# Keys and values projected side by side, outputs moved to the keys' bank, and the engines' orders rewritten, in a fused attention, recurrence and experts layer

## The chip, the cores and the metric

The kernel runs on one core of one Trainium2 chip. The metric is the device time of one execution in microseconds. TensorE, VectorE, ScalarE, GpSimd and SyncE each run their own program; semaphores alone order them.

## What is computed

Three residual stages on 128 sequences of 32 tokens with 256 channels: cross attention over a context of 257 positions per sequence, a short recurrence (its part for sequence 0 is used for all), and a mixture of eight experts of which each token takes two.

```
x = x + xattn(layernorm(x), ctx, mask)       # 16 heads of 16
x = x + attn(layernorm(x), W_in, conv, ...)  # out = Y[0] / norm, norm from cumsums of A * softplus(dt)
x = x + ffn(layernorm(x), router, gate, up, down)

q = hidden @ Wq.T + bq;  k = enc @ Wk.T + bk;  v = enc @ Wv.T + bv
scores = q k / sqrt(16) + mask;  out = softmax(scores) v;  return out @ Wo.T + bo
h = silu(xf @ w_gate[e]) * (xf @ w_up[e]);  out += gates[:, e] * (h @ w_down[e])
```

## The kernel before

The first part (`attend`) covers attention, recurrence and routing, the second (`experts`) the 71 slots of 128 tokens of the experts. The change lies in the first.

A tile is 128 tokens: four sequences, called batches or steps 0 to 3; there are 32 tiles and 128 batches. In step (i, b), batch n = 4i + b, every engine works at several depths: scores and softmax are those of batch n+1, keys and values those of n+2, the split of the context into two parts is that of n+3, and the output is that of n. What follows attention for a whole tile (`i-1`, `i-2`, `i-3`: output projection, norms, softplus, decays, router, ranks) is cut into pieces that hang on a step's number. Tiles 4 to 28 run in a loop on TensorE, the others are unrolled (`steps`, line 278); the order is written out by hand in a function `tile` for each engine (lines 664, 804, 1143, 1291).

TensorE's step before: `scores` of n+1, `project_k` of n+2, `turn_a`, `weigh_values` of n, the first half of `transpose_probs` of n+1, `turn_b`, `project_v` of n+2, the second half of the transposes, `turn_c`. Keys and values are each twelve matmuls of 256 columns of the split (fp32r) type; the others are of 32-bit type. The pieces: `turn_a` is `expand`, `turn_y`, `queries`, `router` for b = 0 to 3; `turn_b` is `sum_decay_and_rank`, `project_y`, `project_dt`, `turn_z1`; `turn_c` is `project_out`, `turn_z2`, `turn_z3`, `sum_a`. All of them write the bank `M`, so each waits until the piece before has been read.

The eight banks of the matmul's memory: `K` (keys), `V_` (values), four `SC` (scores by group), `PT` (transposed probabilities), `M`. The outputs `OT` and the row sums `RP` lie at the end of `SC[0]` (line 228). So scores of n+1 wait for the outputs of n-1 to be taken (`ou_done`, `rp_done`), and weighing waits for the maximum of group 0. Both halves of the transposes use `PT`: the second waits until ScalarE has copied the first.

VectorE: `maxima` (line 879, four per step: scores plus mask, with their row extremum), `take_keys` (868), `take_output` (892, 894), `reciprocals`, and the small operations of the later stages; the softplus is a chain of operations on `dtv` (lines 964 to 984), each waiting for the one before, and ends in `a_done`, for which `sum_a` on TensorE waits. ScalarE: `split_high`, `exponentials` (735), `take_probs`, `take_values`, `take_rp` and the copies out of `M` (711). GpSimd: `split_low` (1249), `lay_queries`, `last_probs` (1267, 1271), the inverse square roots (`power`, 1231 and 1233), table writes. SyncE loads contexts, masks and inputs and is not changed.

## Time and profile before

| | us |
|---|---|
| median of 3 runs | 1527.64 |
| lowest and highest | 1525.33 and 1528.30 |
| the profiled execution | 1529.16 |
| its span | 1527.2 |
| TensorE busy, matmul | 1422.5 (93%) |
| VectorE busy | 1125.5 (74%) |
| ScalarE busy | 1000.9 (66%) |
| GpSimd busy | 838.1 (55%) |
| mean granted TensorE clock | 0.969 of full |

The first scores start at 19.5 us, the last at 956.5; the first expert slot's matmuls start at 1016.5. Between 80 and 110 us the recurrence of sequence 0 is computed once, with TensorE mostly idle. Busy shares are averages over these stages. In the timelines below a line is a run of like instructions: start, busy length, engine, line, operation, output<-inputs and the count; in brackets the idle time ahead of it and what ended it. A matmul's length goes past the start of the next, so the distance of two starts is what a block costs.

### The profile page before, as it was taken

Reading aid. Unit: us, or ns where it says so; the run is one execution under the profiler, and the core shown is the slowest. Engines: PE = TensorE matmul, PEld = TensorE weight load, DVE = VectorE, ACT = ScalarE, POOL = GpSimd, SP = SyncE. Lnnn points to the kernel's source line nnn. Section 1 sums busy time; section 2 is a strip of 40 time slices with the busy share of each in tenths; the row PEclk is TensorE's granted clock in tenths of the full one; section 3 lists DMA queues with packets and bytes.
Section 4 is the critical chain, followed back from the end, with each engine's and each line's share of the span. In section 5 each row is a group of like instructions: output and inputs, shape, how many; then the busy total and the mean of one; then the engine's idle time right before and its main releaser. Section 6 shows DMA issues by size and latency. Waiting matters only on the chain.

```text
span 1527.2 us, 53971 instructions
## 1 busy us (share of the span) xinstructions
PE 1422.5 (93%) x15668; PEld 1294.9 (85%) x15669; DVE 1125.5 (74%) x3967; ACT 1000.9 (66%) x2482; POOL 838.1 (55%) x1401
## 2 busy tenths in 40 slices
PE   6969999999999999999999999649999999999997
PEld 5858888888888888888888888449999999999997
DVE  3647777777777777777777777557877787787775
ACT  4726766767766766766766676237777777677674
POOL 4514655655655655565565554226665666566554
PEclk9969999999999999999999999569999999999999
DMA  5302544554333343343343331425555555556554
GB/s 187 81 12 81 167 140 130 165 159 128 110 103 90 98 114 90 88 119 88 97 117 86 87 81 41 180 78 160 143 162 140 155 145 160 138 144 161 137 141 111
DMA packets 102009, 183.81 MB, mean 120 GB/s; under 512 B 19392, under 2 KB 61376, under 8 KB 101792
## 3 DMA queue, kind: packets, MB, share of 16 engines
q1 hardware_dynamic: 86272, 164.35, 35.2%
q0 software_dynamic: 15680, 18.76, 7.0%
q8 instruction: 29, 0.48, 0.1%
q14 instruction: 28, 0.23, 0.0%
HBM read 152.63 MB, written 31.13 MB: 120 GB/s over the span
## 4 chain that ended last, share of the span: by engine, by line
PE 72%; DVE 8%; issue 6%; ACT 2%; DMA 2%; POOL 1%; POOLq 1%; DVEq 0%; ACTq 0%; SPq 0%
PE m L412 12%; PE k L412 10%; PE y_p L1420 9%; PE v_p L412 9%; PE up_p L1420 8%; PE gate_p L1420 8%; PE sc L412 7%; PE pt L471 5%; PE ht_p L1459 3%; DVE dtv L976 2%; DMA par<-zbuf,gi 2%; ACT wd L735 1%; PE m L493 1%; PE z_p L1426 1%; DVE kT L868 1%
## 5 line engine op out<-in xcount | busy, mean ns | idle before, releaser
L735 ACT ACTIVATE wd<-wd,nmx 128x257 f32<-128x257 f32 x512 | 254.7, 499 | 100.6 <-DVE nmx L879 97.2
L879 DVE CUSTOM_DVE_ANT_0 wd<-sc,wd 128x257 f32<-128x257 f32 x512 | 187.3, 422 | 56.1 <-PE sc L412 45.8
L1622 POOL DMA_INDIRECT out<-par,oi x71 | 113.5, 1599 | 146.7 <-ACT par L1528 146.1
L1249 POOL TENSOR_TENSOR ctx_lo<-wd,ctx_hi 128x516 fp32r<-128x516 f32 x128 | 165.3, 1291 | 48.9 <-ACT ctx_hi L711 44.1
L711 ACT ACTIVATE wd<-pt 128x512 f32<-128x512 f32 x256 | 151.5, 592 | 57.9 <-PE pt L471 57.7
L471 PE MATMUL pt<-con,wd 128*128 128x128 f32 x1024 | 161.0, 280 | 3.0 <-ACT wd L735 0.7
L412 PE MATMUL k<-ctx_hi,wkh 128*128 128x256 f32 x512 | 158.2, 309 | 1.4 <-POOL ctx_lo L1249 1.4
L412 PE MATMUL v_p<-wvh,ctx_hi 128*128 128x256 f32 x512 | 158.0, 309 | 0.5 <-ACT y L711 0.5
L1499 ACT ACTIVATE uw_hi<-wu 128x1408 fp32r x71 | 98.3, 1385 | 85.1 <-PE up_p L1420 84.8
L1610 POOL COPY oi<-par 128x4 int32 x71 | 148.2, 2088 | 0.0
L1557 DVE TENSOR_TENSOR uw_lo<-wu,uw_hi 128x1408 fp32r<-128x1408 f32 x71 | 115.4, 1626 | 41.2 <-ACT uw_hi L1499 41.2
L412 PE MATMUL k<-ctx_lo,wkh 128*128 128x256 f32 x512 | 144.7, 283 | 0.0
L412 PE MATMUL v_p<-wvh,ctx_lo 128*128 128x256 f32 x512 | 144.6, 282 | 0.0
L412 PE MATMUL k<-ctx_hi,wkl 128*128 128x256 f32 x512 | 144.4, 282 | 0.0
L1557 DVE TENSOR_TENSOR gw_lo<-wg,gw_hi 128x1408 fp32r<-128x1408 f32 x71 | 115.4, 1625 | 39.3 <-ACT gw_hi L1499 39.3
L412 PE MATMUL v_p<-wvl,ctx_hi 128*128 128x256 f32 x512 | 143.9, 281 | 0.0
L412 PEld LDWEIGHTS k<-ctx_hi,wkh 128*128 128x128 f32 x512 | 96.4, 188 | 50.5 <-issue 48.7
L1610 POOL COPY gi<-par 128x4 int32 x71 | 122.3, 1722 | 9.5 <-issue 5.7
L1267 POOL TENSOR_TENSOR rr<-wd,rr 128x4 f32<-128x4 f32 x128 | 25.6, 200 | 178.9 <-DVE rr L886 178.9
L1420 PE MATMUL y_p<-wd,hT_hi 128*128 x426 | 121.0, 284 | 1.9 <-DVE hT_lo L1557 1.9
L471 PEld LDWEIGHTS pt<-con,wd 128*128 128x128 f32 x1024 | 113.0, 140 | 10.1 <-ACT wd L735 5.9
L1420 PE MATMUL y_p<-wd,hT_lo 128*128 x426 | 120.4, 283 | 0.0
(197 smaller groups left out, 4662.2 us busy)
## 6 DMA issues: line engine op xcount, KB each, us to landing
dl<-d_low SPq DMA_DIRECT2D x71, 768.0 KB, 4.4
wd<-in_ctx SPq DMA_DIRECT2D x128, 258.0 KB, 2.8
wd<-in_mask SPq DMA_DIRECT2D x512, 32.1 KB, 1.8
wd<-in_wd SPq DMA_DIRECT2D x24, 256.0 KB, 3.0
d_high<-wd SPq DMA_DIRECT2D x24, 256.0 KB, 2.0
d_low<-wd SPq DMA_DIRECT2D x24, 256.0 KB, 2.3
wd<-d_high SPq DMA_DIRECT2D x8, 768.0 KB, 9.1
wg<-in_wg SPq DMA_DIRECT2D x8, 704.0 KB
```

Of the source, the lines that this page charges most:

```text
L412: return nc.tensor.matmul(out, lhsT, rhs, start=start, stop=stop)
L471: last = nc.tensor.transpose(PT[:, o:o + P], pr[:, g, t * P:(t + 1) * P], ident)
L711: return nc.scalar.activation(out, in_, ACT.Copy, **kw)
L735: nc.scalar.activation(pr[:, g, :], sm[:, g, :], ACT.Exp, bias=nmx[:, g:g + 1], scale=-1.0, accum_out=rsum[:, g:g + 1]).then_inc(exp_done, 1)
L879: V.tensor_tensor_reduce(sm[:, g, :], SC[g][:, 0:S], msk[:, b, :], -1.0, 3.0e38, ALU.add, ALU.min, nmx[:, g:g + 1]).then_inc(max_done, 1)
L1249: G.tensor_tensor(ctx_lo[:, b % 2], ctx[:, b], ctx_hi[:, b % 2].bitcast(F32), ALU.subtract).then_inc(lo_done, 1)
L1420: return nc.tensor.matmul(out, lhsT, rhs, start=start, stop=stop)
L1459: last = nc.tensor.transpose(HB[k][:, (c % 4) * P:(c % 4 + 1) * P], hb[:, c * P:(c + 1) * P], ident)
L1499: nc.scalar.activation(dst, src, ACT.Copy).then_inc(done, 1)
L1557: V.tensor_tensor(dst, src, hi.bitcast(F32), ALU.subtract).then_inc(done, 1)
L1610: G.tensor_copy(dst.unsqueeze(1), tab[:, bass.ds(col, 1), :]).then_inc(done, 1)
L1622: G.indirect_dma_start(outd[:, :], bass.IndirectOffsetOnAxis(oi[:, s, 1:2].bitcast(U32), 0), yb[:, s, :], None, compute_op=ALU.add).then_i ...
```

## The change

`OT` and `RP` move to the keys' bank `K`; the second half of the transposes goes to the values' bank `V_`; `px` has two buffers. TensorE's step becomes: `scores`, `turn_c` of the step before, `project_k`, `project_v`, `turn_a`, `weigh_values`, first transposes, `turn_b`, second transposes. The waits follow: keys wait for the outputs of two batches earlier, values for the second half of the probabilities, the second transposes for `v_done`, weighing for `k_done` of batch n+2. VectorE, ScalarE and GpSimd get a new order in `tile`; on VectorE the softplus chain is spread between maxima, keys and heads, `select` and `take_output` are cut into parts for that, and the first statistics change places with the first residual.

```diff
-        px = sb("px", [P, 2, NH, NG, 2])
+        px = sb("px", [P, 2, 2, NH, NG, 2])
...
-        OT = SC[0][:, SP:SP + NH * 2 * Q].rearrange("p (a h q) -> p a h q", a=NH, h=2)
-        RP = SC[0][0:2 * H, SP + NH * 2 * Q:SP + NH * 2 * Q + Q]
+        OT = K[:, 0:NH * 2 * Q].rearrange("p (a h q) -> p a h q", a=NH, h=2)
+        RP = K[0:2 * H, NH * 2 * Q:NH * 2 * Q + Q]
...
                 at_least(pe, k_done, 2 * n)
+                at_least(pe, ou_done, n - 2)
+                at_least(pe, rp_done, n - 2)
...
                 at_least(pe, v_done, n)
+                at_least(pe, pt_done, 2 * n - 2)
...
                 at_least(pe, max_done, 4 * n)
-                at_least(pe, ou_done, n - 1)
-                at_least(pe, rp_done, n - 1)
...
                 pe.wait_ge(exp_done, 4 * n + 2 * d + 2)
-                at_least(pe, pt_done, 2 * n + d)
+                at_least(pe, pt_done, 2 * n)
+                if d and runs(following(i, b)[0]):
+                    pe.wait_ge(v_done, n + 2)
...
-                        last = nc.tensor.transpose(PT[:, o:o + P], pr[:, g, t * P:(t + 1) * P], ident)
+                        last = nc.tensor.transpose((PT, V_)[d][:, o:o + P], pr[:, g, t * P:(t + 1) * P], ident)
...
-                if runs(nxt[0]):
-                    pe.wait_ge(max_done, 4 * n + 5)
+                if runs(following(i, b, 2)[0]):
+                    pe.wait_ge(k_done, 2 * n + 6)
...
                     if runs(nxt[0]):
                         scores(*nxt)
+                    turn_c(*((i, b - 1) if b else (i - 1, TB - 1)))
                     if runs(two[0]):
                         project_k(*two)
+                        project_v(*two)
                     turn_a(i, b)
                     if runs(i):
                         weigh_values(i, b)
                     if runs(nxt[0]):
                         transpose_probs(*nxt, 0)
                     turn_b(i, b)
-                    if runs(two[0]):
-                        project_v(*two)
                     if runs(nxt[0]):
                         transpose_probs(*nxt, 1)
-                    turn_c(i, b)
...
```

ScalarE's step after (`tile`, its first lines are unchanged):

```diff
+                    if b == 2 and runs(i - 1):
+                        keep(i - 1)
                     if runs(nxt[0]):
-                        exponentials(*nxt, 0, 1, 2)
...
+                        exponentials(*nxt, 0)
+                    if b == 0 and runs(i - 2):
+                        decays(i - 2)
+                    if b == 2 and runs(i - 1):
+                        take_z2T(i - 1)
+                    if b == 3 and runs(i - 2):
+                        take_z3T(i - 2)
...
+                        exponentials(*nxt, 1, 2, 3)
...
+                    if runs(two[0]):
+                        take_values(*two)
+                    if b == 1 and runs(i - 2):
+                        take_ynT(i - 2)
+                    if runs(nxt[0]):
+                        take_probs(*nxt, 0)
+                    if b == 3 and runs(i + 2):
+                        take_z1T(i + 2)
+                    if b != 0 and runs(i):
+                        take_rp(i, b)
+                    if runs(nxt[0]):
+                        take_probs(*nxt, 1)
+                    if b == 0 and runs(i):
+                        take_rp(i, b)
...
```

VectorE's step after, whole (a plus marks a new or moved line; the lines taken away are left out):

```diff
             def tile(i):
                 for b in range(TB):
                     nxt, two = following(i, b), following(i, b, 2)
+                    soft_now = b == 3 and runs(i - 1)
+                    pick_now = b == 3 and runs(i - 2)
+                    if runs(nxt[0]):
+                        maxima(*nxt, 0, 1)
+                    if soft_now:
                         softplus_ratio(i - 1)
+                    if runs(nxt[0]):
+                        maxima(*nxt, 2)
+                    if soft_now:
                         softplus_series(i - 1, 0, 1)
                     if runs(nxt[0]):
+                        maxima(*nxt, 3)
+                    if b == 1 and runs(i - 1):
+                        residual1(i - 1)
+                    if b == 2 and runs(i - 2):
+                        normalise3(i - 2)
+                    if soft_now:
+                        softplus_series(i - 1, 1, 2)
+                    if runs(two[0]):
+                        take_keys(*two, 0)
+                    if soft_now:
+                        softplus_series(i - 1, 2, 3)
+                    if runs(two[0]):
+                        take_keys(*two, 1)
+                    if b == 1 and runs(i - 1):
+                        statistics2(i - 1)
+                    if soft_now:
+                        softplus_series(i - 1, 3, 4)
                     if runs(nxt[0]):
+                        reciprocals(*nxt)
+                    if soft_now:
+                        softplus_series(i - 1, 4, len(ATANH))
+                    if b == 0 and runs(i + 2):
+                        statistics1(i + 2)
                     if b == 0 and runs(i - 1):
                         weigh(i - 1)
+                        attention_out(i - 1)
+                    if b == 1 and runs(i - 3):
+                        place(i - 3)
+                    if b == 1 and runs(i - 1):
+                        normalise2(i - 1)
                     if b == 2 and runs(i + 1):
                         take_queries(i + 1)
+                    if pick_now:
                         take_logits(i - 2)
+                    if soft_now:
+                        softplus_log(i - 1)
+                    if pick_now:
+                        select_top(i - 2)
+                    if soft_now:
+                        softplus_sum(i - 1)
                     if runs(i):
+                        first_head(i, b)
+                    if pick_now:
+                        select_index(i - 2)
+                    if runs(i):
+                        second_head(i, b)
+                    if soft_now:
                         softplus_end(i - 1)
+                    if pick_now:
+                        select_number(i - 2)
+                        select_one_hot(i - 2)
+                        select_both(i - 2)
                     if b == 0 and runs(i - 2):
                         norms(i - 2)
                     if b == 0 and runs(i - 3):
                         take_ranks(i - 3)
                     if b == 0 and isinstance(i, int) and i == 2:
                         ssd()
+                    if b == 0 and runs(i - 2):
+                        scale_y(i - 2)
                     if b == 1 and runs(i - 2):
                         residual2(i - 2)
                     if b == 2 and runs(i - 1):
                         soft_in(i - 1)
```

GpSimd:

```diff
-                at_least(pool, o_ready, n)
+                at_least(pool, o_ready, n - 1)
                 for k in range(2):
-                    G.tensor_tensor(px[:, k, :, :, :].rearrange("p a g h -> p g a h"),
+                    G.tensor_tensor(px[:, b % 2, k].rearrange("p a g h -> p g a h"),
...
                     if b == 2 and runs(i - 2):
                         power(2, i - 2, mv3, var3, rstd3)
+                    if b != 2 and runs(two[0]):
+                        lay_queries(*two)
+                    if runs(three[0]):
+                        split_low(*three)
+                    if b == 0 and runs(i - 1):
+                        add_bias(i - 1)
+                    if b == 2 and k is not None:
+                        piece_low(k)
+                    if runs(nxt[0]):
+                        last_probs(*nxt)
                     if b == 1 and runs(i - 1):
                         power(1, i - 1, mv2, var2, rstd2)
-                    if runs(three[0]):
-                        split_low(*three)
-                    if runs(two[0]):
+                    if b == 2 and runs(two[0]):
                         lay_queries(*two)
-                    if runs(nxt[0]):
-                        last_probs(*nxt)
-                    if b == 0 and runs(i - 1):
-                        add_bias(i - 1)
                     if b == 2 and runs(i + 2):
                         normalise1(i + 2)
-                    if b == 2 and k is not None:
-                        piece_low(k)
                     if b == 3 and runs(i - 3):
                         write_slots(i - 3)
```

## Rows read from the trace of the kernel before

**Rows 1.** Busy time of each engine from 400 to 700 us; the columns are named as printed.
```profile
400.00:700.00 300.00, 287.82 (x3872) 251.14 (x3865) 233.84 (x1127) 207.08 (x638) 174.82 (x361) 1.00 0.35 98
```

**Rows 2.** Timeline of TensorE, one loop tile: start, us, line, out<-in, count.
```profile
508.07 0.69 PE L412 MATMUL sc<-kT,qbd 32*64 32x257 f32 x16 [0.54 <-issue]
508.69 0.38 PE L412 MATMUL k<-ctx_hi,wkh 128*128 128x256 f32 x1
...
510.24 1.05 PE L412 MATMUL m<-rp,con 128*128 128x128 f32 x8
...
511.69 0.22 PE L412 MATMUL sc<-con,px 128*32 128x32 f32 x2
511.85 0.66 PE L471 MATMUL pt<-con,wd 128*128 128x128 f32 x4
512.34 0.29 PE L412 MATMUL m<-dtv,con 128*128 128x16 f32 x2
...
512.93 0.36 PE L412 MATMUL v_p<-wvh,ctx_hi 128*128 128x256 f32 x1
513.13 0.28 PE L412 MATMUL v_p<-wvl,ctx_hi 128*128 128x256 f32 x1
...
514.43 0.60 PE L471 MATMUL pt<-con,wd 128*128 128x128 f32 x4
...
515.83 0.69 PE L412 MATMUL sc<-kT,qbd 32*64 32x257 f32 x16
...
518.79 0.22 PE L412 MATMUL sc<-con,px 128*32 128x32 f32 x2
519.07 0.66 PE L471 MATMUL pt<-con,wd 128*128 128x128 f32 x4
519.83 1.13 PE L412 MATMUL m<-par,ynT 128*128 128x256 f32 x4
...
529.85 0.69 PE L412 MATMUL sc<-kT,qbd 32*64 32x257 f32 x16
...
536.26 0.37 PE L412 MATMUL m<-dtv,con 128*128 128x16 f32 x2 [0.46 <-DVE dtv L984]
537.21 0.66 PE L412 MATMUL sc<-kT,qbd 32*64 32x257 f32 x11 [0.58 <-issue]
```

**Rows 3.** Waits of TensorE, 110 to 1050 us: us in total, times, longest.
```profile
PE m L412 <- DVE dtv L984: 16.4, 28, 2.5
PE sc L412 <- issue: 14.8, 27, 0.8
```

**Rows 4.** Timeline of TensorE, the end of an unrolled tile, same columns.
```profile
941.46 0.37 PE L412 MATMUL m<-dtv,con 128*128 128x16 f32 x2 [0.35 <-DVE dtv L984]
941.80 0.69 PE L412 MATMUL sc<-kT,qbd 32*64 32x257 f32 x16
```

**Rows 5.** Timeline of VectorE in the same loop tile.
```profile
517.30 0.43 DVE L879 CUSTOM_DVE_ANT_0 wd<-sc,wd 128x257 f32<-128x257 f32 x1
...
518.69 0.87 DVE L868 TENSOR_SCALAR kT<-k,par 128x256 f32<-128x256 f32 x2
519.48 0.27 DVE L892 TENSOR_SCALAR om<-sc,own 128x64 f32<-128x64 f32 x1
...
522.23 0.14 DVE L1053 TENSOR_REDUCE sv<-ohr 128x2 f32<-128x16 f32 x1
...
523.46 0.43 DVE L899 BATCH_NORM_STATS2 st<-wd 128x6 f32<-128x256 f32 x1
...
534.05 1.44 DVE L976 SCALAR_TENSOR_TENSOR dtv<-dtv 128x16 f32<-128x16 f32 x6
```

**Rows 6.** Timeline of GpSimd in the same loop tile.
```profile
517.24 0.19 POOL L1231 TENSOR_TENSOR rs<-mv,con 128x1 f32<-128x1 f32 x1 [1.68 <-DVE mv L901]
...
518.07 1.27 POOL L1249 TENSOR_TENSOR ctx_lo<-wd,ctx_hi 128x516 fp32r<-128x516 f32 x1
```

**Rows 7.** Timeline of ScalarE in the same loop tile.
```profile
511.02 0.49 ACT L735 ACTIVATE wd<-wd,nmx 128x257 f32<-128x257 f32 x1
```

87 lines of the change are left out of this document (24 added, 63 removed).

## The prediction

> **What bounds the kernel now.** The profiled execution spans 1527.2 us and took 1529.2 us in all; the median of the runs is 1527.64, so this execution lies 1.5 us above it. In the stretch from 400 to 700 us, all of it tiles of the attention loop, TensorE matmuls are busy 287.8 of 300 us at the full granted clock, VectorE 233.8, ScalarE 207.1, GpSimd 174.8, and the DMA engines a third of the time. [rows 1] Matmul records overlap, so I do not trust the busy share; I read the order of starts. In the timeline of TensorE one loop tile (four batches, called steps 0 to 3 below) runs from the scores at 508.07 to those at 537.21: 29.14 us. Blocks follow each other without a hole except in three places. [rows 2] In step 3 TensorE waits 0.46 us for `a_done`, does two matmuls of `sum_a`, then starts the next scores 0.58 us late, with nothing but "issue" as the cause. The waits of TensorE over the whole attention part say the same: 16.4 us in 28 waits for VectorE's line 984 and 14.8 us in 27 for "issue" before the scores. [rows 3] The second is the loop's turn: behind a wait that ended late, branch and register waits stand in the open. In an unrolled tile the scores follow `sum_a` after 0.34 us (941.46 to 941.80) where the loop takes 0.95 (536.26 to 537.21). [rows 2, 4] The third place is step 1: the last matmul of the outputs to the first transpose takes 0.28 us where step 0 takes 0.16, and transposes to the next block take 0.76 where step 0 takes 0.49. [rows 2] That is 0.12 + 0.27 = 0.39 us, behind maxima that VectorE starts 1.47 us after the scores (515.83 to 517.30), late because it still did the first residual and its statistics. [rows 2, 5]
> So TensorE's program order is the bound, and what can be won is the stalls in it: 0.46 + 0.58 + 0.39 = 1.43 us of 29.1 per tile, with whatever changes between blocks cost.
>
> **The change part by part.**
> *Keys and values adjacent.* The first value matmul behind a 32-bit one takes 0.20 us to the next start (512.93 to 513.13), the other eleven (514.43 - 513.13) / 11 = 0.118. [rows 2] Behind the keys, of the same type, I expect 0.118: 0.08 us less per batch, 0.32 per tile. The keys keep their own such first matmul. Bounds: no gain at all, and twice as much.
> *`sum_a` (all of `turn_c`) behind the next scores.* The wait for `a_done` now has scores in front of it (0.62 us, 508.07 to 508.69) and the second transposes too. VectorE must finish its six `dtv` operations, 1.44 us in a row today, and three more of about 0.2. [rows 2, 5] The new order breaks that row up between maxima, keys and heads, where each waits less. I lay VectorE out for step 3 from the scores' start: maxima from 0.83 (as in an undelayed step), 1.39 for four (517.30 to 518.69), keys 0.79 (518.69 to 519.48), ratio and series about 1.9 in between and after (nine operations of 0.21), logits, logarithm, maximum and heads 1.4: `a_done` near 6.3. [rows 5] Without stalls step 3 lasts 7.36 - 1.04 - 0.08 = 6.24, and `sum_a` is reached at 6.24 + 0.62 = 6.86. Slack 0.5: the 0.46 goes.
> *The loop's turn.* Its 0.58 was open because TensorE had just been released. Now the last late wait ahead of it is that of `turn_z1` for the logits, near 5.1, and transposes of 0.31 and 0.44 stand between. Branch and waits took about 0.9 (536.26 to 537.21), so the scores could be ready to issue near 6.3 against 6.24: I keep 0.1 open. Bounds: 0 and 0.6.
> The Trainium skill ("Runtime: NRT & Kernel Launch", section on instruction fetch mechanics) says that a taken branch to a target outside the window must fetch it before going on. By that rule the gap would be there wherever the wait stands, the 0.5 just taken would stay, and the loop's 25 turns would keep 12 us. The trace shows the gap only behind a late wait, so it can't tell the two apart; this is rival 1.
> *Outputs in the keys' bank.* Weighing batch n now waits until VectorE has taken the keys of n+2 (`k_done`), for it writes their bank; it no longer waits for the maxima of group 0, and scores no longer wait for the outputs of n-1. Behind that wait on TensorE stand the weighing, both transposes and `turn_b`; ScalarE's copies and VectorE's heads wait for these. Keys are copied 0.79 us; they are ready k-block 1.55 + 0.15 after its start (508.69 to 510.24). Step 0: TensorE reaches the weighing at 0.62 + 0.3 + 1.55 + 1.4 + 1.0 = 4.85, keys are taken by 3.6. Step 1: 4.85 against 4.25. Step 2: 4.85 against 4.0. Step 3: with the router's four small matmuls, put at 0.4, 4.3, keys (maxima 1.39, three ratio operations 0.6, series 0.3, keys 0.79, behind 0.83) 4.2, and the semaphore and register waits behind it bring 0.15. [rows 2, 5] Sum: 0.15 per tile. From below nothing is to be had here; above, all of VectorE's lateness counts once per step.
> The Trainium skill ("PSUM — Partial Sum Buffer", section on bank collisions) has two engines on one bank and quadrant as an error, not a slowdown. It speaks against this part: the wait can't be loosened by using other columns of the bank. No row here shows it, and it adds no term.
> *Keys' bank, other side.* Projecting the keys of n+2 waits for the outputs (`ou_done`) and rows (`rp_done`) of n-1. Behind it stand both projections. ScalarE copies the rows of step 0 after its second transposes, near 7.8, that is 0.9 into step 1; the keys start at 1.6. In the other steps the slack is 0.5 or more. Cost 0.
> *Second transposes in the values' bank.* They wait for `v_done` of n+2 in place of ScalarE's copy of the first half; values are ready at about 4.1, copied in 0.6, and these transposes start at 5.7 or later. Projecting values waits for the copy of n's second half, which ended 2 us before. Cost 0, and the old wait was hidden as well (transposes 514.43 follow values without a hole). [rows 2]
> *VectorE, step 1.* `residual1` and `statistics2` come here, `statistics1` goes to step 0. In order: maxima, residual, keys, statistics, reciprocals, placement 1.23 (522.23 to 523.46), normalise, heads, second residual. [rows 5] From 0.83 that sums to 7.6 for the second residual, done at 8.0, where step 2 begins at 7.36 and `turn_z2` wants it at 7.98. Cost 0.15. It removes the 0.39, for `turn_y`'s copy now waits only for the projection before it. The start of step 2's maxima slips about 0.5, which weighing at 4.85 does not feel.
> *ScalarE.* It takes the values before the first half of the probabilities; both have an idle stretch before them today, and no step fills it: per step four exponentials, three copies and the split, about 4.6 of 6.4 us at least. Cost 0.
> *GpSimd, step 1.* Its two `power` operations today start 1.41 us into the step (515.83 to 517.24). [rows 2, 6] They move behind splitting and `last_probs`, which waits for the reciprocals at about 5.1 (behind VectorE's statistics; the last exponential starts 2.95 us into a step today, 508.07 to 511.02): 0.7 for the probabilities' three operations, an estimate, then 0.83 for `power` (517.24 to 518.07), done near 6.7. [rows 2, 6, 7] Normalising on VectorE is reached at 6.3, so 0.4 is lost there; this is in the 7.6 above. GpSimd's table writes and SyncE's loads keep their places; the earlier split of the contexts only adds slack. `px` doubled frees GpSimd from waiting for the outputs before. Cost 0.
> *Sum.* A loop tile: 29.14 - 0.46 - 0.58 - 0.39 - 0.32 + 0.15 (`k_done`) + 0.15 (`x2_done`) + 0.1 (turn) = 27.8, a gain of 1.35. TensorE loops 25 tiles: 33.8 us. Outside the loop five tiles (2, 3, 29 to 31) have no turn to lose and less to win, 0.7 each: 3.5. Tiles 0 and 1 have eight adjacent pairs: 0.6. The pass that computes the recurrence once (tile 2) now copies values after it: +0.6. The tail of the attention part and the experts are untouched; that VectorE and ScalarE meet the tail's steps in another order I put at 0, between -1 and +1. Together 37.3 us: 1529.2 - 37.3 = 1491.9 in this execution's terms, 1.5 less for the median: 1490.4, say 1490.
>
> **The rivals.**
> 1. *The turn of the loop stays, and half of the small stalls come back.* The gap of 0.58 would stand in every loop tile: 25 x 0.5 = 12.5, and 0.3 more per tile (7.5) for register waits between the many short blocks. Time 1502 to 1512, centre 1508. For it: the only unrolled turn shown has no branch at all. [rows 4] Against it: TensorE's work ahead of the branch is not held up any more.
> 2. *More than I count.* The change of type also costs at the keys behind scores, k_done and x2_done never bind, no turn shows: 25 x 1.75 + 5 x 1 + 1 = 50, time 1478, or to 1474 if adjacency is worth twice 0.08.
> 3. *Slower: GpSimd's `power` in step 1.* One chain: exponentials, reciprocals, `last_probs`, `power`, VectorE's normalising, heads, second residual, then TensorE's `turn_z2` and the next maxima. Whatever it is late stands on TensorE once per tile. At 6.7 it costs nothing more; late by 1.5 us the gain of 1.35 is gone, late by 2 us the tile takes 29.8 and the kernel 1527.6 + 25 x 0.65 - 4 = 1540. For it: three engines hand over in turn, and VectorE has 6.6 of 7.4 us to do in this step, so lateness isn't absorbed. Against it: nothing in GpSimd's own queue between the split and `last_probs` is long enough.
> 4. *The stall only moves:* `a_done` is as late against the new `sum_a` as before, and `k_done` eats the rest: within 0.2% of before.
>
> **How the numbers follow.** The forecast, 1478 to 1502, has a chance of 0.60; rival 1 0.18; rival 2 0.07; rival 3 0.10; rival 4 0.05. About 0.2% (3 us) is what a measurement of this kernel can tell from no change. Faster: 0.60 + 0.18 + 0.07 = 0.85; the same 0.05; slower 0.10. The range reaches over rival 1 and most of rival 2, from 1476 to 1513, and leaves out rivals 3 and 4 and some edges.
>
> **What the profile after would show.** In TensorE's timeline value matmuls start 0.12 us behind the keys' last, in all loop batches; scores follow the second transposes with at most 0.1 of "issue"; no wait of `sum_a` for line 984; a loop tile of 27.8 us with steps near 7.1, 7.3, 6.9 and 6.4. Step 3 longer than 6.9 means that the turn or `k_done` binds (the first as "issue" before scores, the second as VectorE's keys before the weighing). A wait for the second residual before `turn_z2` above 0.5 us, and maxima of step 2 over 1 us late, mean rival 3. I am wrong as a whole if the loop tile is over 28.6 us, or if the time moved in the experts' part.

## The result and the profile after

The changed kernel takes 1550.74 us (median of 4 runs, 1550.11 to 1553.27), the kernel before 1527.97 beside it (4 runs, 1525.33 to 1530.07): a ratio of 1.0149, interval 1.0133 to 1.0165. It is slower by 22.8 us, where 1490 was forecast and 1476 to 1513 given as range. The profiled execution took 1550.11 us, with a span of 1548.1.

Busy time of each engine, 400 to 700 us, the columns of [rows 1]:

```profile
400.00:700.00 300.00, 280.54 (x3823) 243.20 (x3823) 239.95 (x1112) 204.33 (x628) 170.81 (x355) 1.00 0.35 100
```

The clock is the same 1.00. TensorE does less in the same stretch (280.5 us busy, 287.8 before), so it waits more. The distance from one step's first scores to the next one's, as the median of the 25 loop tiles, worked out from the starts of the matmuls, gives the place (us; the kernels e1 to e9 and e11 to e13 are those of the experiments, and their rows are explained there):

| kernel | step 0 | step 1 | step 2 | step 3 | loop tile | last scores | median of runs |
|---|---|---|---|---|---|---|---|
| before | 7.76 | 7.15 | 6.87 | 7.32 | 29.10 | 956.5 | 1527.97 |
| after | 7.06 | 7.96 | 6.79 | 7.77 | 29.59 | 979.9 | 1550.74 |
| e1, split behind the product | 7.06 | 7.97 | 6.79 | 7.95 | 29.77 | 992.3 | 1567.47 |
| e2, four value buffers | 7.05 | 7.25 | 6.83 | 7.41 | 28.55 | 947.3 | 1520.13 |
| e3, both | 7.05 | 7.25 | 6.87 | 7.55 | 28.72 | 954.8 | 1526.61 |
| e4, turned y copied first | 7.05 | 7.25 | 6.83 | 7.78 | 28.91 | 959.3 | 1535.06 |
| e5, softplus behind the keys | 7.06 | 7.96 | 6.79 | 6.92 | 28.72 | 950.9 | 1522.82 |
| e6 = e2 + e5 | 7.05 | 7.25 | 6.87 | 6.89 | 28.06 | 929.7 | 1501.87 |
| e9 = e6, logits earlier | 7.42 | 7.26 | 6.84 | 6.38 | 27.91 | 926.4 | 1497.02 |
| e12 = e9, heads last | 7.90 | 7.26 | 6.84 | 6.34 | 28.34 | 938.7 | 1509.26 |
| e13 = e9, weighing first | 7.05 | 7.51 | 6.83 | 6.33 | 27.73 | 923.2 | 1494.80 |
| e11 = e9, `turn_c` back | 8.19 | 7.43 | 6.83 | 7.61 | 30.07 | 996.0 | 1566.72 |
| e7, split that only writes | 7.05 | 7.96 | 6.79 | 7.00 | 28.80 | 955.4 | 1524.31 (one run) |
| e8 = before, values moved | 10.41 | 7.04 | 7.70 | 8.52 | 33.67 | 1084.7 | 1654.49 |

Since `turn_c` went from the end of a step to behind the next scores, a step of before and one of after don't hold the same work; the tile does. After: 0.49 us more per loop tile (12 us), and 0.8 to 2.2 us more in each of the tiles outside the loop (tile 0 took 22.4 us and takes 24.2, tile 1 went from 25.7 to 27.9, tile 2 from 56.6 to 57.4, tile 3 from 28.4 to 29.3, tiles 29 and 30 from 28.0 to 29.7 and 29.4). The first scores start at 19.5 us before and at 21.1 after, and between 19.6 and 22.6 us in the experiments; this offset stands in the column of the last scores too, and no run here explains it. From the last scores to the end it is 568.2 us (570.7 before): the experts' part has nothing to do with it.

TensorE's waits from 110 to 1060 us, as in [rows 3]: us in total, times, longest:

```profile
PE k L412 <- DVE kT L871: 29.7, 25, 1.2
PE m L412 <- ACT ynT L712: 14.2, 32, 0.5
...
PE sc L412 <- issue: 3.9, 24, 0.2
PE m L412 <- DVE dtv L999: 3.8, 2, 2.0
```

The two large waits of before are nearly gone, as forecast: `sum_a`'s for `a_done` (line 984 before, 999 now) from 16.4 us to 3.8, and the loop's turn from 14.8 us to 3.9. [rows 3] Two new ones stand in their place: in step 3 the weighing waits 1.2 us for the keys that VectorE takes, in step 1 `turn_y` waits 0.44 for ScalarE's copy. Both in TensorE's timeline (columns as in [rows 2]):

```profile
513.76 0.69 PE L412 MATMUL sc<-kT,qbd 32*64 32x257 f32 x16
...
516.10 0.28 PE L412 MATMUL v_p<-wvh,ctx_hi 128*128 128x256 f32 x1
...
517.51 0.51 PE L412 MATMUL m<-par,z3T 128*128 128x8 f32 x4
519.21 0.65 PE L412 MATMUL k<-wd 128*32 128x64 f32 x32 [1.20 <-DVE kT L871]
...
521.54 0.69 PE L412 MATMUL sc<-kT,qbd 32*64 32x257 f32 x16 [0.16 <-issue]
...
535.07 1.13 PE L412 MATMUL m<-par,ynT 128*128 128x256 f32 x4 [0.44 <-ACT ynT L712]
```

Why VectorE is late with the keys of step 3: its timeline, and GpSimd's beside it.

```profile
514.60 0.43 DVE L882 CUSTOM_DVE_ANT_0 wd<-sc,wd 128x257 f32<-128x257 f32 x1 [0.75 <-PE sc L412]
514.95 0.42 DVE L882 CUSTOM_DVE_ANT_0 wd<-sc,wd 128x257 f32<-128x257 f32 x1
515.30 0.40 DVE L974 TENSOR_SCALAR dtv<-dtv 128x16 f32<-128x16 f32 x1
515.73 0.26 DVE L975 RECIPROCAL dtv<-dtv 128x16 f32<-128x16 f32 x1
516.02 1.07 DVE L976 TENSOR_TENSOR dtv<-dtv 128x16 f32<-128x16 f32 x1
517.01 0.41 DVE L882 CUSTOM_DVE_ANT_0 wd<-sc,wd 128x257 f32<-128x257 f32 x1
...
518.68 0.48 DVE L871 TENSOR_SCALAR kT<-k,par 128x256 f32<-128x256 f32 x1
```

```profile
515.27 0.39 POOL L1305 TENSOR_TENSOR qbd<-wd,own 128x128 f32<-128x128 f32 x1
515.61 0.18 POOL L1309 COPY kT<-wd 128x4 f32 x1
515.76 1.30 POOL L1297 TENSOR_TENSOR ctx_lo<-wd,ctx_hi 128x516 fp32r<-128x516 f32 x1
```

A product of sixteen numbers per partition takes 1.07 us, and it ends (517.09) with GpSimd's split (517.06). In the groups of lines from 153 to 900 us it is so in every loop tile, while the next operation of the same shape takes a sixth of it:

```profile
L976 DVE TENSOR_TENSOR dtv<-dtv 128x16 f32<-128x16 f32 x25 | 26.7, 1070 | 0.9
...
L982 DVE TENSOR_TENSOR dtv<-dtv 128x16 f32<-128x16 f32 x25 | 4.2, 166 | 0.0
```

And why ScalarE is late in step 1: it stands idle for 1.47 us before it copies the values, released by the weighing (TensorE's `k<-wd`), and the turned y (`ynT`) comes behind that copy.

```profile
532.06 0.62 ACT L712 ACTIVATE wd<-wd 128x512 fp32r<-128x512 f32 x1
534.14 0.60 ACT L712 ACTIVATE wd<-v_p 128x512 f32<-128x512 f32 x1 [1.47 <-PE k L412]
534.63 0.38 ACT L712 ACTIVATE ynT<-m 128x256 f32<-128x256 f32 x1
```

### The profile page after: what moved, and what is told of

It reads as the page before. It is cut to its first block, busy times and chain, and to the rows that moved or that the text cites. A ratio compares the mean times of both kernels' runs of the same rounds, so it can differ in the third digit from the quotient of the medians.

```text
span 1548.1 us, 54247 instructions
## 1 busy us (share of the span) xinstructions
PE 1418.1 (92%) x15668; PEld 1284.6 (83%) x15669; DVE 1159.3 (75%) x3967; ACT 1000.2 (65%) x2482; POOL 833.5 (54%) x1401
## 4 chain that ended last, share of the span: by engine, by line
PE 76%; issue 7%; DVE 5%; DMA 2%; ACT 2%; POOL 1%; DVEq 0%; POOLq 0%; ACTq 0%; SPq 0%
PE k L412 14%; PE m L412 12%; PE y_p L1470 9%; PE v_p L412 8%; PE up_p L1470 8%; PE gate_p L1470 8%; PE sc L412 5%; PE v_p L474 4%; PE pt L474 3%; PE ht_p L1509 3%; PE m L495 2%; DMA par<-zbuf,gi 2%; PE z_p L1476 1%; DVE kT L871 1%; ACT ynT L712 1%
## 5 line engine op out<-in xcount | busy, mean ns | idle before, releaser
L712 ACT ACTIVATE wd<-v_p 128x512 f32<-128x512 f32 x256 | 152.8, 597 | 234.9 <-PE k L412 193.4
L882 DVE CUSTOM_DVE_ANT_0 wd<-sc,wd 128x257 f32<-128x257 f32 x512 | 191.8, 422 | 69.8 <-PE sc L412 65.0
L412 PE MATMUL v_p<-wvh,ctx_hi 128*128 128x256 f32 x512 | 143.5, 280 | 0.0
L871 DVE TENSOR_SCALAR kT<-k,par 128x256 f32<-128x256 f32 x256 | 114.2, 478 | 31.3 <-PE k L412 30.8
L1470 PE MATMUL y_p<-dl,hT_hi 128*128 128x256 f32 x426 | 119.9, 282 | 0.0
L412 PE MATMUL k<-wd 128*32 128x64 f32 x4096 | 84.1, 223 | 36.3 <-DVE kT L871 29.7
```

What stands on the lines that cost most here:

```text
L412: return nc.tensor.matmul(out, lhsT, rhs, start=start, stop=stop)
L712: return nc.scalar.activation(out, in_, ACT.Copy, **kw)
L871: V.tensor_scalar(kT[:, b % 2, a, 0:LAST], K2[:, a, :], prm("bk")[:, a:a + 1], None, ALU.add).then_inc(k_done, 1)
L882: V.tensor_tensor_reduce(sm[:, g, :], SC[g][:, 0:S], msk[:, b, :], -1.0, 3.0e38, ALU.add, ALU.min, nmx[:, g:g + 1]).then_inc(max_done, 1)
L1470: return nc.tensor.matmul(out, lhsT, rhs, start=start, stop=stop)
```

## The experiments

The theory after these readings had two causes. *First*, the softplus product reads two operands in SBUF, the on-chip memory that VectorE and GpSimd both work from, while GpSimd's split reads there as well; it waits until the split has ended, and maxima, keys and weighing wait behind it. The Trainium skill ("SBUF — State Buffer", section "Who interferes with whom") says that such a VectorE instruction contends with a GpSimd instruction that reads SBUF, not with one that only writes; its summary adds that the second to issue blocks fully until the first has finished. The rows above agree: the product starts 0.26 us behind the split and ends 0.03 us after it. *Second*, `take_values` waits until batch n has been weighed (`o_ready`), since there are two value buffers; now that the values are ready before the weighing, that wait stands in the open. The rivals: the order of VectorE's operations alone is too long for step 3; ScalarE is late because of what was put ahead of its copies; or GpSimd's `power` in step 1 (rival 3).

All ratios are to the kernel before, run beside the experiment, with their 95% intervals. Differences in us are between medians; the kernel before had 1527.97 to 1529.42 us beside these runs (1535.80 beside e12), so a difference of one or two us says nothing.

**e1. GpSimd's split waits for the product.**

```diff
+                    if b == 3 and runs(i - 1):
+                        pool.wait_ge(soft, NSOFT * (i - 1) + 3)
                     if runs(three[0]):
                         split_low(*three)
```

> The changed kernel with one wait more: in step 3 GpSimd splits the context of batch n+3 only after VectorE's two-input product of the softplus (line 976). In the changed kernel's trace that product lasts 1.07 us (0.17 in the kernel before) and ends with GpSimd's split (515.76 to 517.06 us), and weighing in step 3 waits 1.26 us for the keys. Theory A, the product is held up by GpSimd's split: it falls back to 0.17 us, step 3 from 7.77 to about 6.8 us, the loop tile from 29.6 to about 28.6, the kernel from 1551 to about 1526 us. Theory B, VectorE simply has too much in a row in step 3 and the long record is only how a wait shows: the product stays long or another wait of the same size stands there, the time stays within 5 us of 1551.

Measured: 1567.47 us, 1.0254 (1.0237 to 1.0271), 17 us slower than the changed kernel. The product is free, but the next operation with two operands of that memory is caught in its place. Groups of lines, 153 to 900 us:

```profile
L982 DVE TENSOR_TENSOR dtv<-dtv 128x16 f32<-128x16 f32 x25 | 27.7, 1109 | 0.0
...
L976 DVE TENSOR_TENSOR dtv<-dtv 128x16 f32<-128x16 f32 x25 | 4.4, 176 | 0.9
```

What follows: the long time doesn't belong to the instruction but to what GpSimd does beside it; and keeping one instruction clear of the split is no cure as long as the chain lies between maxima and keys. The weighing now waits 1.4 us for the keys (33.8 us in 25 waits). That is 0.18 us more per loop tile, 4.5 of the 17 us. In two of the 25 loop tiles, the step after such a wait takes 9.7 and 9.8 us where the others take 7.06, at a lower granted clock (columns as in [rows 1]); that makes 5 us more in the profiled execution, and in the median run, which is 6.7 us longer, the granted clock is lower still (0.963 and less over the execution, 0.964 in the profiled one). The rest lies in tiles 1 and 2.

```profile
707.55:717.33 9.78, 9.78 (x99) 8.69 (x98) 4.98 (x21) 4.63 (x15) 4.40 (x10) 0.68 0.25 65
```

**e2. Four value buffers.**

```diff
-            v = part(2 * TC * D).rearrange("p (b t d) -> p b t d", b=2, t=TC)
+            v = part(4 * TC * D).rearrange("p (b t d) -> p b t d", b=4, t=TC)
...
-                at_least(act, o_ready, n - 1)
-                copy(v[:, b % 2, :, :]
+                at_least(act, o_ready, n - 3)
+                copy(v[:, b, :, :]
```

> The changed kernel with four buffers for the values in place of two, so that ScalarE's copy of the values of batch n+2 no longer waits until batch n is weighed. Theory A, this wait, which the order values before weighing brings, delays ScalarE in every step and causes the 0.6 us for which TensorE waits for the turned y in step 1 (copied behind the values), and the longer steps of tiles 0 and 1 (5.75 against 5.32 us): step 1 falls from 7.96 to about 7.4, steps of tile 0 to 5.3, the kernel by 25 x 0.6 + 5 x 0.6 + 8 x 0.4 = 21 us to about 1530. Theory B, the 0.6 us come from the late maxima of step 1: no change in step 1, the time within 5 us of 1551.

Measured: 1520.13 us, 0.9939 (0.9923 to 0.9956): 30.6 us off the changed kernel and already faster than before. The wait for `ynT` is gone from the list; the one for the keys stands untouched at 29.7 us in 25. Step 1 falls by 0.71, five of the eight steps of tiles 0 and 1 by 0.40 to 0.46 each, and step 3 by 0.36. In step 3 too the values' copy stood behind the weighing; there the second transposes, which write the bank it reads, waited for it: from `turn_z1` to them it takes 0.42 us in the changed kernel (520.33 to 520.75) and 0.21 in e2, and the 0.16 us of "issue" behind them are gone as well. So the second cause is real, and it is worth more than its row in the list of waits (14.2 us) says, for the row names only the one place where the lateness met TensorE as a single long gap.

**e3. Both of them.** The edits of e1 and e2 together.

> Both edits together. If both theories A hold and the two stalls are independent, the loop tile falls from 29.6 to 28.6 - 0.6 = 28.0 or a little under and the kernel to 1500 to 1510 us, faster than both kernels. If the one stall only hides the other, the gain is that of the larger one alone, about 1526.

Measured: 1526.61 us, 0.998 (0.9969 to 0.9991). Step 3 is longer than e2's by about as much as e1's was than the changed kernel's (7.55 in place of 7.41, with the same 33.8 us of waits for the keys): the two causes act side by side. The kernel loses only 6.5 us against e2, where e1 lost 17; no loop tile of e3 shows the lower clock.

**e4. ScalarE copies the turned y ahead of the values.** Only the order, the buffers stay two.

```diff
+                    if b == 1 and runs(i - 2):
+                        take_ynT(i - 2)
                     if runs(two[0]):
                         take_values(*two)
-                    if b == 1 and runs(i - 2):
-                        take_ynT(i - 2)
```

> The changed kernel with two ScalarE operations exchanged in step 1: the turned y is copied before the values, still with two value buffers. Theory A of the value buffers: the copy of y no longer stands behind the wait for weighing, the 0.6 us in step 1 go to at most 0.2 and the kernel gains 10 to 17 us, while the steps of tiles 0 and 1 stay at 5.75. Theory B, late maxima: no change.

Measured: 1535.06 us, 1.0034 (1.0019 to 1.0048). Step 1 is cured by this alone (7.25, the same as with four buffers): the cause there is what stands behind the waiting copy, not ScalarE's load. Step 3 and the first tiles keep what e2 took away, 15 us.

**e5. VectorE's softplus behind the keys.** In step 3 all four maxima first, then both halves of the keys, then ratio and series in a row.

```diff
                     if runs(nxt[0]):
-                        maxima(*nxt, 0, 1)
-                    if soft_now:
-                        softplus_ratio(i - 1)
-                    if runs(nxt[0]):
-                        maxima(*nxt, 2)
-                    if soft_now:
-                        softplus_series(i - 1, 0, 1)
-                    if runs(nxt[0]):
-                        maxima(*nxt, 3)
+                        maxima(*nxt, 0, 1, 2, 3)
...
                     if runs(two[0]):
-                        take_keys(*two, 0)
...
-                        take_keys(*two, 1)
+                        take_keys(*two, 0, 1)
...
+                    if soft_now:
+                        softplus_ratio(i - 1)
+                        softplus_series(i - 1, 0, 4)
```

> The changed kernel with VectorE's step 3 in another order: all four maxima and both key copies first, the softplus chain behind them in one piece. GpSimd's split (2.0 to 3.3 us into the step) then lies beside maxima and key copies, which take their main input from the matmul's banks. Theory A (a two-input operation is held up while GpSimd's split runs): no product over 0.2 us, the keys are ready at about 3.2 us and TensorE's wait of 1.2 us before weighing is gone; a_done comes about 0.2 us later than the next sum_a; step 3 from 7.77 to 6.5 to 6.7, the kernel to 1551 - 25 x 1.15 = 1522 us. Theory B (too much work in step 3): the wait moves to sum_a in full and the time stays near 1551.

Measured: 1522.82 us, 0.9966 (0.9954 to 0.9979), 28 us off the changed kernel. Step 3 falls from 7.77 to 6.92 us, the product takes 0.18, and no wait for the keys is listed. The softplus chain ends later now and something else becomes last, TensorE's waits from 110 to 1060 us:

```profile
PE m L412 <- ACT ynT L712: 14.2, 32, 0.5
PE m L495 <- DVE lg L1038: 11.9, 28, 0.5
```

The copy of the logits stands behind series and reciprocals in VectorE's order, and `turn_z1` waits for it.

**e6. Four buffers and the softplus behind the keys.** The edits of e2 and e5.

> The edit of e5 together with the four value buffers of e2 (1520 us). Both stalls of the changed kernel are then taken away and nothing else is changed. If the prediction missed only these two, the loop tile is 27.3 to 27.7 us and the kernel 1520 - 25 x 1.1 = 1492 us, the time that was predicted for the change itself. If another wait stands behind them, the tile stays over 28 us.

Measured: 1501.87 us, 0.9827 (0.9808 to 0.9846): 49 us off the changed kernel. The parts brought 30.6 and 27.9; they don't add up. The 0.36 us that four buffers took from step 3 are not there a second time (6.92 us in e5, 6.89 here): once the keys are early, `turn_z1` waits for the logits (11.9 us in 28, the same in e5 and e6), and the values are copied under that wait. A loop tile takes 28.06.

**e7. A split that only writes.** GpSimd sets the low part for batch 2 of each tile to zero (all but four columns), where it subtracted; the order of the changed kernel is kept.

```diff
                 pool.wait_ge(hi_done, n + 1)
+                if b == 2:
+                    G.tensor_tensor(ctx_lo[:, b % 2, :, 0:4], ctx[:, b, :, 0:4], ctx_hi[:, b % 2, :, 0:4].bitcast(F32),
+                                    ALU.subtract)
+                    G.memset(ctx_lo[:, b % 2, :, 4:SP].bitcast(F32), 0.0).then_inc(lo_done, 1)
+                    return
                 G.tensor_tensor(ctx_lo[:, b % 2], ctx[:, b], ctx_hi[:, b % 2].bitcast(F32), ALU.subtract
```

> The changed kernel with the split of the context of batch 2 of each tile (the one that runs in step 3) replaced by an operation of GpSimd that writes zeros and reads nothing, behind a subtraction of four columns; this leaves the low part of that context out of keys and values. GpSimd is busy at the same time as before, but hardly reads. If it is GpSimd's reading that holds up VectorE's two-input product, the product at line 976 falls to about 0.2 us and step 3 loses about 0.9 us; if any GpSimd operation at that time does it, or if it has nothing to do with GpSimd, the product stays at 0.9 us or more.

Measured: 1524.31 us in one execution; step 3 takes 7.00 us in place of 7.77. GpSimd, and below it VectorE:

```profile
503.69 0.20 POOL L1298 TENSOR_TENSOR ctx_lo<-wd,ctx_hi 128x8 fp32r<-128x8 f32 x1
503.83 0.52 POOL L1300 MEMSET ctx_lo<- 128x508 f32 x1
```

```profile
503.22 0.40 DVE L974 TENSOR_SCALAR dtv<-dtv 128x16 f32<-128x16 f32 x1
503.66 0.26 DVE L975 RECIPROCAL dtv<-dtv 128x16 f32<-128x16 f32 x1
503.95 0.18 DVE L976 TENSOR_TENSOR dtv<-dtv 128x16 f32<-128x16 f32 x1
```

The product starts and ends inside the writing operation (503.83 to 504.35) and takes 0.18 us. So it is not GpSimd's being busy that holds it, nor the order of VectorE's operations, which is unchanged; what the edit took away is the other engine's reading. That agrees with what the Trainium skill says above. But not every reading operation does it. In the kernel before, the same product ran inside GpSimd's `power` in all 26 tiles from 150 to 900 us, an operation with two operands of one column, and took 0.17 us each time:

```profile
529.62 0.55 POOL L1233 TENSOR_TENSOR rs<-rs,con 128x1 f32<-128x1 f32 x1
529.80 0.17 DVE L966 TENSOR_TENSOR dtv<-dtv 128x16 f32<-128x16 f32 x1
```

So the full blocking of the later operation is seen here beside the split of 516 columns and not beside an operation of one column; where between them it begins no run shows.

The rival, that the order alone is too long for step 3, is not wholly wrong either. In e7 the weighing still waits 0.42 us per tile for the keys (10.4 us in 25, before 29.7): of the 1.19 us, 0.77 are the product's and 0.42 come from the softplus operations that stand between maxima and keys. Only e5, which moves them all, takes the whole wait away.

The operation before the product, one operand and a scalar (`L974`), still takes 0.40 while GpSimd multiplies `qbd` (503.20 to 503.59); the same section of the Trainium skill counts this kind among those that can take the shared ports in a mode of their own, and this row is in line with it.

**e8. The kernel before with its values moved behind the keys, and nothing else.**

```diff
                     if runs(two[0]):
                         project_k(*two)
+                        project_v(*two)
                     turn_a(i, b)
...
                     turn_b(i, b)
-                    if runs(two[0]):
-                        project_v(*two)
```

> The kernel before with one part of the change alone: project_v directly behind project_k, everything else (banks, other orders, ScalarE's order) as before. The saving of the adjacent types is 4 x 0.08 = 0.3 us per tile, 8 us in all. Against it: both halves of the transposes still share a bank, and now only turn_b stands between them, so the second half waits for ScalarE's copy of the first (0.6 us and the way there) in steps with a short turn_b: at least 0.3 us in steps 2 and 3, 15 us or more. Expected 1535 to 1550, slower than before, if the bank is what the other parts of the change are for; 1518 to 1522 if adjacency can be had alone.

Measured: 1654.49 us, 1.0819 (1.0797 to 1.0841): 125 us slower than the kernel before beside it, far outside both expectations. TensorE's waits from 110 to 1060 us:

```profile
PE m L412 <- DVE dtv L983: 26.6, 28, 1.0
PE pt L471 <- ACT wd L710: 23.7, 59, 0.6
PE m L412 <- DVE chosen L1044: 19.1, 28, 0.7
PE sc L412 <- issue: 13.9, 26, 0.6
```

The 1.5 us of value matmuls between the halves of the transposes were the cover for the copy of the first half and for VectorE's later operations. Without them, and without the second bank and the moved `turn_c`, these lie open: 83.3 us listed, where before had 31.2. [rows 3] A second loss comes on top, the clock. Stretches of one such place, then step 0 of two other loop tiles, then the mean (columns as in [rows 1]):

```profile
636.50:639.50 3.00, 1.07 (x7) 0.72 (x6) 2.56 (x18) 2.15 (x8) 0.59 (x3) 1.00 0.83 252
639.50:646.00 6.50, 6.46 (x76) 5.98 (x80) 1.90 (x10) 2.63 (x9) 3.83 (x5) 0.74 0.44 103
239.73:250.16 10.43, 9.62 (x100) 8.39 (x100) 4.99 (x23) 4.99 (x15) 5.24 (x9) 0.84 0.55 181
273.43:282.34 8.91, 8.10 (x100) 6.87 (x100) 5.04 (x23) 5.04 (x15) 5.25 (x9) 1.00 0.66 214
400.00:700.00 300.00, 269.92 (x3385) 228.70 (x3384) 201.74 (x982) 181.36 (x559) 153.25 (x316) 0.96 0.32 92
```

For three microseconds TensorE is busy for 1.07; then it works without a hole and its mean granted clock is 0.74. In the timeline the keys' matmuls start 0.21 us apart (641.14, 641.35, 641.56) where it is 0.118 in [rows 2]: the lower of the two levels, 1.2 in place of 2.4 GHz. The third and fourth stretch are step 0 of two loop tiles: in 18 of the 25 it takes 10.4 us at a clock of 0.84, in the other seven 8.9 us at full clock, which makes 27 us. Over 400 to 700 us the clock is 0.96; 4% of the 1063 us between first and last scores, 43 us, are the most that it can have cost in all. With the 52 us more of listed waits that makes 79 to 95 of the 125 us; the rest I could not assign, it lies in gaps that the list doesn't show.

**e9. The logits earlier.** e6, with their copy ahead of the softplus' last part.

```diff
+                    if pick_now:
+                        take_logits(i - 2)
                     if soft_now:
                         softplus_series(i - 1, 4, len(ATANH))
...
-                    if pick_now:
-                        take_logits(i - 2)
```

> e6 (1501.9 us) with one more move on VectorE: the router's logits are read behind the fourth term of the softplus series and not behind the seventh. In e6 TensorE waits 0.5 us per tile for that reading before it turns z1 (11.9 us in 28 waits). If this is the last stall of its kind, the wait is gone, step 3 falls from 6.89 to about 6.4 us, the loop tile to 27.6 and the kernel to 1490 us. If the softplus chain behind it then stands in the way (a_done later than the next sum_a), the gain is half or less, 1495 to 1502.

Measured: 1497.02 us, 0.9791 (0.9772 to 0.9811). The wait for the logits is gone, step 3 takes 6.38 us, 0.51 less; but step 0 takes 0.37 more. Of a gain of 0.51 per tile 0.15 is left. The time lies where the second expectation had it, but not for its reason: TensorE's list from 153 to 900 us has 1.0 us of waits for `a_done`, in three waits. e12 and e13 look for the reason.

**e11. e9 with `turn_c` back at the end of its step.**

```diff
                         scores(*nxt)
-                    turn_c(*((i, b - 1) if b else (i - 1, TB - 1)))
...
                         transpose_probs(*nxt, 1)
+                    turn_c(i, b)
```

> e9 with turn_c (project_out, turn_z2, turn_z3, sum_a) put back at the end of its own step on TensorE, all else as in e9. The prediction gave 1.04 us per tile to this move: the wait of sum_a for a_done and the loop's turn in the open behind it. If that price is right the loop tile is 1.0 to 1.3 us longer than e9's and the kernel 25 to 33 us slower than e9, about 1518; if the move is worth nothing, the two are the same.

Measured: 1566.72 us, 1.024 (1.0222 to 1.0258), 70 us slower than e9, far more than I had thought. TensorE's waits:

```profile
PE m L412 <- DVE dtv L999: 27.8, 31, 2.1
PE m L495 <- DVE x L1019: 18.4, 31, 0.6
PE sc L412 <- issue: 11.0, 25, 0.5
...
PE m L412 <- issue: 7.4, 29, 0.3
```

In e9's order of the other engines the place behind the scores hides `sum_a`'s wait, that of `turn_z2` for the second residual, and the loop's turn. Since e11 keeps that order, with the softplus late in the step, its 70 us are the price of the place under the new order, and no measurement of the 1.04 us per tile that the prediction gave to it under the old one. The lower clock has a small part: step 0 takes 9.7 us in three loop tiles and 8.2 in the others.

**e12. The heads last.** e9, and in step 3 VectorE sends the choice of the expert and the last softplus operation ahead of the output's two copies.

```diff
+                    if pick_now:
+                        select_index(i - 2)
+                    if soft_now:
+                        softplus_end(i - 1)
                     if runs(i):
                         first_head(i, b)
-                    if pick_now:
-                        select_index(i - 2)
-                    if runs(i):
                         second_head(i, b)
-                    if soft_now:
-                        softplus_end(i - 1)
```

> The kernel with four value buffers, the softplus product behind the keys' copy and the logits earlier (1497 us), and in step 3 VectorE sends the choice of the chosen expert and the last softplus operation ahead of the two copies of the output's heads. In that kernel the weights' sum of step 0 waits 0.37 us per tile for VectorE, and nothing else in the tile waits for VectorE for longer than that. If this wait is paid by the two copies that stand ahead of it in VectorE's order, 25 loop tiles and the four unrolled ones save 0.3 us each, some 8 us: 1489, with step 0 at 7.1 us in place of 7.42. If the copies of the heads, now later, hold back the bank of the next keys, the wait only moves to the keys of step 0 and the time stays within 2 us of 1497. What it can't show is whether any of it comes from GpSimd.

Measured: 1509.26 us, 0.9827 (0.9805 to 0.9849); the kernel before took 1535.8 on that chip, so by the ratios it is 0.4% slower than e9. Both expectations missed, and the premise was wrong: in e9's timeline `sum_a` follows the scores after 0.63 us, without a wait. What step 0 lost was, for the most part, the gap to the sum of the decays. That gap, in e9 and below in e12 (TensorE):

```profile
527.73 0.66 PE L474 MATMUL pt<-con,wd 128*128 128x128 f32 x4
528.50 0.40 PE L412 MATMUL m<-dtv,con 128*128 128x16 f32 x2
```

```profile
534.09 0.66 PE L474 MATMUL pt<-con,wd 128*128 128x128 f32 x4
535.09 0.40 PE L412 MATMUL m<-dtv,con 128*128 128x16 f32 x2 [0.34 <-DVE t L930]
```

It is 0.77 in e9 and 1.00 in e12; 0.49 is what the same distance takes in the changed kernel (526.96 to 527.45). Of the 0.37 us that e9 lost in step 0 this is 0.28, and 0.11 more lie between this block's start and the next (0.25, in the changed kernel 0.14). The same bank is being read by VectorE's `weigh` (`t`, line 930). In e12 VectorE also ends step 3 0.46 us later against the scores, and step 0's keys, which write the bank that the heads read, start 0.48 us behind `sum_a`, not 0.24. 0.23 and 0.24 are the 0.47 that step 0 grew by. That the late heads hold the keys is read from the order of the rows, not tried.

**e13. The weighing first.** e9, and in step 0 VectorE does the two products of `weigh` ahead of the statistics of the next input.

```diff
+                    if b == 0 and runs(i - 1):
+                        weigh(i - 1)
                     if b == 0 and runs(i + 2):
                         statistics1(i + 2)
                     if b == 0 and runs(i - 1):
-                        weigh(i - 1)
                         attention_out(i - 1)
```

> The kernel with four value buffers, the softplus product behind the keys' copy and the logits earlier (1497 us), and in step 0 VectorE sends the two products of the attention weights and the outputs (weigh) ahead of the statistics of the next input. In that kernel no wait of step 0 is printed, but on TensorE the start of the first transposes to the sum of the decays takes 0.77 us (527.73 to 528.50) where the same distance without a wait is 0.49 to 0.50, and the second product, which reads the same bank, ends at 528.45. The statistics that stand before the products take 0.61 us (527.08 to 527.69), the products' own input is there at about 527.1. If this is the 0.37 us that step 0 is longer than its floor, the products end 0.6 us earlier, step 0 goes from 7.42 to about 7.15, and 28 tiles save 0.27 each: 7.5 us, 1489 to 1490. If something else holds step 0 (the copy of the heads, which stays where it is), 1497.

Measured: 1494.80 us, 0.9779 (0.9753 to 0.9805), the fastest of all and 2.2% below the kernel before, though its interval and e9's overlap. Step 0 falls by 0.37 to 7.05, as the theory had it; but step 1 rises by 0.25, for `project_out`, now reached earlier, has to wait for what still reads its bank:

```profile
525.90 0.66 PE L474 MATMUL pt<-con,wd 128*128 128x128 f32 x4
526.39 0.29 PE L412 MATMUL m<-dtv,con 128*128 128x16 f32 x2
...
527.54 0.69 PE L412 MATMUL sc<-kT,qbd 32*64 32x257 f32 x16
528.44 1.10 PE L412 MATMUL m<-par,aT 128*128 128x256 f32 x4 [0.21 <-issue]
```

The gap of the decays is down to 0.49 (525.90 to 526.39), and 0.9 us lie between scores and projection where there were 0.62 (529.76 to 530.38 in e9). VectorE's last reader of the bank, `chosen`, ends at 528.33; the row itself names no releaser, so this cause is argued and not shown. The step from e9 to e13 was to bring 7.5 us and brought about 2, which the two intervals can't tell from nothing; the loop tile is 0.18 us shorter.

## Why the prediction was wrong

The forecast summed a loop tile of 27.8 us; it took 29.59. Two steps failed: the term for `k_done`, put at 0.15 us per tile, where TensorE waited 1.19, and "ScalarE, cost 0", which cost 1.0 us per tile. Term by term:

- *Where TensorE's stalls are and what they cost* was right. `sum_a`'s wait and the turn went, by 0.46 and 0.42 us per tile. Rival 1, that the turn stays whatever stands before it, is refuted: 0.16 us of "issue" are left, where 0.1 were forecast, and in e2 and e6 the loop's turns show next to none (one gap of 0.2 us in e6, none in e2, 153 to 900 us).
- *Keys and values adjacent* was right in size: the twelve value matmuls take 1.41 us (516.10 to 517.51), 1.50 before [rows 2], so 0.09 per batch and 0.36 per tile, 0.32 forecast. e8 shows what the sum didn't say, that this small gain gives up a cover of 1.5 us.
- *Outputs in the keys' bank, `k_done`, +0.15* is the first step that failed. I put VectorE's keys in step 3 at 4.2 us and TensorE at the weighing at 4.3; the terms that I gave for the keys add up to 3.9 only. TensorE was there at 4.2; the keys ended at 5.4 (513.76 to 519.16). The maxima began at 0.84, as forecast; the "three ratio operations 0.6" took 1.71 from the start of the first to that of the next maximum (515.30 to 517.01). I took their duration from a place of the old order, where GpSimd's split didn't run beside them (there product 529.80, split from 532.77), and never laid GpSimd's timeline beside VectorE's. The split's row stood in front of me, 1.27 us long. [rows 6] Even with a product of 0.18 us the term was too small: e7 leaves 0.42 us of wait per tile, and the first of the three ratio operations alone is 0.23 us longer than before (0.40 in place of 0.17).
- *ScalarE, cost 0* is the second. I counted its work (4.6 of 6.4 us) and not its waits. The line that I read past is `at_least(act, o_ready, n - 1)`: before, the values came after the weighing, and the wait was free; the change puts the values ahead of the weighing, and with two buffers it can't be free. e2 and e4 show the price: 0.71 in step 1, 0.36 in step 3 as long as the keys are late there, and 0.40 to 0.46 in five steps of tiles 0 and 1.
- *The logits near 5.1* were late too: once both causes are gone (e6), `turn_z1` waits 0.42 us per tile for them, as 11.9 us in 28 waits show.
- *`x2_done`, +0.15* shows nowhere: in e2 and e6 TensorE's list from 153 to 900 us has no wait for the second residual.
- *Tiles 0 and 1: a gain of 0.6.* They lost 1.8 and 2.2 us. Tile 0 lost them by ScalarE's wait: with four buffers it takes 22.6. Tile 1 takes 27.2 with four buffers and 25.5 once the softplus has moved too, so most of its loss was the first cause.
- *Five tiles outside the loop: 0.7 each.* They lost like the others (tile 3 1.0 us, tiles 29 and 30 1.7 and 1.4). Tile 2, with the recurrence, lost 0.8. TensorE is not mostly idle in the recurrence's stretch, as I wrote: from 80 to 110 us it is busy for 20.0 us, at a granted clock of 0.54.
- *Rival 3* had the right side and the wrong mechanism. `power` in step 1 is nowhere last: with four buffers step 1 takes 7.25 with the same GpSimd order, where the forecast had 7.3.
- *Rival 4* named the right place, `k_done` of step 3 eating what the moved `sum_a` wins, but at a price of nothing more than the gain.

With the two failed terms mended (e6) the tile takes 28.06 us and with the logits 27.91, 0.1 from the sum; and the kernel 1497.0, 7 us over the forecast. That it comes so close is luck in part: the two waits of 0.15 us each are not in e9's list, and 0.37 us in step 0, which the sum didn't have, stand in their place. So the sum held where it was read from rows, and the two terms that I had put at 0.15 and 0 cost 49 us and the logits 5: a gain of 31 us became a loss of 23.

## What to carry to other kernels

When small operations of one engine are moved between its large ones, lay the other engine's timeline beside the new places, above all VectorE's operations with two operands in SBUF beside GpSimd's elementwise ones: the old duration holds only at the old place. When a block is moved ahead of another, look up every buffer wait of those who read it, for a wait that cost nothing was hidden by the old order; and read the first repair's trace for the next wait, since 28 and 31 us of two repairs gave 49 together, and a gain of 0.37 us in step 0 gave 0.25 back in step 1.

## What the hardware showed unexpectedly

- A 128x16 product with two SBUF operands takes 0.17 to 0.18 us alone (e6) and 1.07 to 1.11 beside GpSimd's 1.30 us subtraction of 516 columns; beside a GpSimd memset it takes 0.18 (e7), and beside a GpSimd operation on two operands of one column 0.17 (before).
- VectorE's operation with one operand and a scalar is lengthened too: `L974` takes 0.40 beside GpSimd's multiplications and 0.17 elsewhere (e6: 0.16); the normalisation of 128x256 at line 1027 takes 0.68 in e9 and 0.80 in the changed kernel, where the one at line 1033 takes 0.41. The second pair is seen only, not tried.
- After three microseconds with a third of its time busy, TensorE fell to the lower clock level (e8); sixteen matmuls 0.213 us apart in place of 0.118 cost some 1.5 us. Stalls of the same kind end every loop tile of e8; step 0 behind them was slow in 18 of 25 and not in the other seven. In e1, where each loop tile has a wait of 1.4 us, the clock fell behind two of 25, at 2.7 us each; in the changed kernel, with waits of 1.2 us, behind none.
